# A four-layer decoder on one core: cross-attentions with queries on the partitions, new heads and ends of the expert layers, one context product

## The reference

```python
# l0x and l3x: 16 heads of 8 features, 512 queries against 77 context rows
Q, K, V = split_heads(x @ Wq + bq), split_heads(ctx @ Wk + bk), split_heads(ctx @ Wv + bv)
scores = jnp.einsum('bhqd,bhkd->bhqk', Q, K) / jnp.sqrt(8)     # l0x: mask == 0 -> -1e9 (no biases)
out = merge_heads(jnp.einsum('bhqk,bhkd->bhqd', softmax(scores), V)) @ Wo + bo
# l2x: 8 heads of 64; keys are the 77 context rows (masked) and the 512 tokens
k, v = split(concatenate([ln_x(ctx), ln_l(x)]) @ w_kv); q = ln_l(x) @ w_q * 64 ** -0.5
out = ln_o(merge(softmax(q @ k.T) @ v) @ w_out)
# l1f: top 2 of 8 experts of unlike kinds (width 512), weights by the softmax of nx @ router_w, nx = ln(x)
# l3f: top 2 of 8 experts, weights by the softmax of the two logits, and a shared expert for every token:
shared_out = (silu(x @ sw1) * (x @ sw3)) @ sw2                  # 2 slices of 128
moe_out = sum over the chosen e of cw[e] * ((silu(x @ w1[e]) * (x @ w3[e])) @ w2[e])
```

## Time and profile before

| | us |
|---|---|
| median of 3 runs | 2277.38 (2273.33 to 2279.63) |
| profiled execution | 2252.73 |
| its span, mean granted clock | 2250.9, 0.899 |
| l0x | 158 to 302 |
| l1f | 667 to 1083 |
| l2x | 1155 to 1557 |
| l3x | 1939.9 to 2081.9 |
| l3f | 2082.4 to 2250.9 |
| busy: PE, DVE, ACT, POOL | 1797.8, 1477.1, 1048.0, 393.3 |

### The profile page before, as it was taken

The page is one execution under the profiler, slowest core; times in us unless marked ns, Lnnn a source line. Parts: engine busy times, 40 slices in busy tenths (PEclk is TensorE's granted clock), DMA queues, the critical chain, the costliest instruction groups (busy, mean ns, idle before and its releaser), DMA issues. The chain is left out here.

```text
span 2250.9 us, 34926 instructions
## 1 busy us (share of the span) xinstructions
PE 1797.8 (80%) x12404; PEld 1094.5 (49%) x12521; DVE 1477.1 (66%) x3404; ACT 1048.0 (47%) x2229; POOL 393.3 (17%) x575
## 2 busy tenths in 40 slices
PE   5768967999965999995779999993489889687872
PEld 3445542343334566663556666662245444344661
DVE  4436757888846555555546677686879999566524
ACT  2325534777721333332526555551167777365221
POOL 0110021000023444443110000001200000100374
PEclk8879977999975999998879999996589999799896
DMA  3000000000015588884000000000000000000373
GB/s 86 0 1 1 1 1 0 1 1 1 1 54 212 211 301 300 297 298 146 1 1 1 1 1 1 1 1 17 0 1 2 1 1 2 1 1 1 110 216 115
DMA packets 42797, 134.65 MB, mean 60 GB/s; under 512 B 7117, under 2 KB 22529, under 8 KB 37443
## 3 DMA queue, kind: packets, MB, share of 16 engines
q1 hardware_dynamic: 36587, 121.17, 15.5%
q0 software_dynamic: 4992, 10.23, 1.5%
q10 hardware_dynamic: 1048, 1.01, 0.2%
HBM read 123.29 MB, written 11.45 MB: 60 GB/s over the span
## 5 line engine op out<-in xcount | busy, mean ns | idle before, releaser
L153 POOL TENSOR_SCALAR rstd<-MV 128x2 f32<-128x2 f32 (+1 forms) x100 | 24.4, 244 | 1109.2 <-DVE MV L125 1102.6
L845 DVE TENSOR_REDUCE l1aM<-PS 128x2 f32<-128x1024 f32 x128 | 152.8, 1220 | 22.9 <-PE PS L601 20.8
L763 ACT ACTIVATE l1aE<-PS 128x512 f32<-128x512 f32 x256 | 140.9, 595 | 49.0 <-PE PS L630 45.6
L1575 PE MATMUL PS<-WB,H 128*128 128x512 f32 x312 | 142.6, 600 | 1.2 <-ACT H L1692 1.2
L763 ACT ACTIVATE l3aE<-PS 128x512 f32<-128x512 f32 (+3 forms) x256 | 102.5, 443 | 47.6 <-PE PS L634 44.9
L2463 DVE TENSOR_REDUCE M<-PS 128x1 f32<-128x589 f32 x128 | 92.5, 764 | 36.0 <-PE PS L2274 36.0
L845 DVE TENSOR_REDUCE l3aM<-PS 128x2 f32<-128x256 f32 (+3 forms) x128 | 101.3, 819 | 20.6 <-PE PS L603 19.6
L2372 ACT COPY PT<-PS 128x512 f32<-128x512 f32 x128 | 69.1, 590 | 92.9 <-PE PS L2285 92.6
L2378 ACT ACTIVATE E<-PS,M 128x589 f32<-128x589 f32 x128 | 95.8, 761 | 22.7 <-DVE M L2463 22.6
L1692 ACT ACTIVATE H<-PS,WB 128x128 f32<-128x128 f32 x156 | 44.5, 368 | 121.3 <-PE PS L1566 121.3
L873 DVE SCALAR_TENSOR_TENSOR l3aE<-l3aE,l3aLB 128x2048 f32<-128x2048 f32 (+1 forms) x64 | 94.9, 1483 | 2.7 <-ACT l3aE L763 2.7
(11 more groups left out here) (695 smaller groups left out, 4666.6 us busy)
## 6 DMA issues: line engine op xcount, KB each, us to landing
WB<-in_experts SPq DMA_DIRECT2D x39, 1798.0 KB
TB<-mixed_tails SPq DMA_DIRECT2D x39, 384.0 KB
WB<-in_experts SPq DMA_DIRECT2D x39, 384.0 KB, 4.2
WB<-mixed_out SPq DMA_DIRECT2D x8, 256.0 KB, 4.8
YB<-expert_out SPq DMA_DIRECT2D x8, 256.0 KB, 4.7
WB<-in_fold SPq DMA_DIRECT2D x1, 1676.0 KB, 7.0
cols_l2x_sb<-in_cols_l2x SPq DMA_DIRECT2D x1, 1154.0 KB, 10.2
mixed_tails<-in_tails SPq DMA_DIRECT2D x1, 1152.0 KB, 8.7
```

The costliest lines, as they stand in the source:

```text
L763: nc.scalar.activation(E[0:kn, home(m, kt) + j, q0:S], PS[0:kn, 4 + n % 2, q0:S], ACT.Exp, scale=SCALE).then_inc(exp_done, 1)
L845: v.tensor_reduce(M[:, m % 2, qt, 2 * hp:2 * hp + 2], PS[:, bank:bank + 2, 0:kc], AX, ALU.max, negate=True).then_inc(pair_free, 1)
L1575: mm(o, H1[:, i % 3, c * P:(c + 1) * P], mid_w(i, c), start=(c == 0), stop=False)
```

## The change

**1. l0x and l3x** call a new function, `cross_attention`. Queries are on the partitions. Keys of a batch are spread into `KS`, in which each of eight slots of 77 columns keeps only one head's rows; a score unit S is four float32 matmuls of 64 queries with 308 columns (four heads of 77), one in each quadrant of the array. VectorE takes the maximum and adds it, ScalarE the exponential over 616 columns, X transposes it (8 per unit), O multiplies with V and a column of ones (nine moving columns per head), and VectorE divides. The mask is added on PE by two bf16 matmuls. Nothing is gathered or split.

```diff
+CROSS = (
+    (("X", 1, 0, 0), ("X", 1, 0, 1), ("S", 2, 0), ("O", 0), ("X", 1, 1, 0), ("X", 1, 1, 1), ("S", 2, 1)),
...
+def cross_attention(k, name, w, mask=None):
...
+                        if mask is not None:
+                            mm(PS[:, 2 * (n % 2) + g, 0:CW], k.ident_b, mask[:, qt:qt + 1, :].broadcast_to([P, HG, SC]), start=True, stop=False,
...
+                    for half in range(2):
+                        for g in range(2):
+                            c0, rows = qt * P + 64 * half, slice(64 * g, 64 * g + 64)
+                            ins = mm(PS[64 * half:64 * half + 64, 2 * (n % 2) + g, 0:CW], Q[rows, b % 2, c0:c0 + 64],
+                                     KS[rows, b, HG * p:HG * p + HG, :].rearrange("p j n -> p (j n)"), start=mask is None, stop=True,
...
+                elif kind == "X":
...
+                    for j in range(HG):
+                        ins = nc.tensor.transpose(PS[0:SC, 4 + g, j * P:(j + 1) * P], E[:, n % 2, g, j, :], k.ident)
...
+                    for p in range(2):
+                        for g in range(2):
+                            for j in range(HG):
+                                h = HG * (p + 2 * g) + j
+                                ins = mm(PS[:, 6, h * DA:(h + 1) * DA], ET[:, (2 * i + p) % 4, HG * g + j, :], Va[:, b, h, :], start=True, stop=True)
...
+                    v.tensor_reduce(top[:, s], sc, AX, ALU.max, negate=True).then_inc(maxed, 1)
...
+                    v.tensor_tensor(E[:, s], sc, top[:, s].unsqueeze(3).broadcast_to([P, 2, HG, SC]), ALU.add).then_inc(shifted, 1)
...
-            attention16(k, "l0x", W["l0x"], k.CT, (mask_b[:, :, :], maskT_b[:, :]))
+            cross_attention(k, "l0x", W["l0x"], mask_b[:, :, :])
...
-            attention16(k, "l3x", W["l3x"], k.CT)
+            cross_attention(k, "l3x", W["l3x"])
```

```diff
+            pe.wait_ge(marked, 1)
+            disp.count_tensor(COUNTS, counted)
             pe.wait_ge(centred, 2)
-            pe.wait_ge(scaled, 3)
+            pe.wait_ge(scaled, 2)
...
-            pe.wait_ge(marked, 1)
-            disp.count_tensor(COUNTS, counted)
-            pe.wait_ge(spread, 1)
             pe.wait_ge(lowered, 1)
-            disp.list_tensor(LIST, listed)
+            disp.list_tensor(pe, LIST, spread, listed)
...
+            act.wait_ge(fold_in, 16)
+            for q in range(8):
+                ins = nc.scalar.mul(gd[:, q, :], fold["down"][:, q * P:(q + 1) * P], fold["g1"][:, q:q + 1])
+            ins.then_inc(scaled, 1)
...
+        step(v.tensor_tensor(self.high[:, :, :], self.at_tile[:, :, :],
+                             self.ids_b[:, :].unsqueeze(2).broadcast_to([P, 2 * N, T]), ALU.mult))
+        for c in range(2):
+            own = slice(c * N, (c + 1) * N)
+            v.tensor_tensor(self.at_row[:, own, :], self.iota_b[:, :].unsqueeze(1).broadcast_to([P, N, P]),
+                            self.row_b[:, own].unsqueeze(2).broadcast_to([P, N, P]), ALU.is_equal).then_inc(spread, 1)
```

```diff
+    shared = [u for b in range(BT) for u in (("up", b, 0), ("up", b, 1), ("down", b, 0), ("down", b, 1))]
+    between = {2 * n: u for n, u in enumerate(shared)}
...
+                if i in between and i:
+                    what, b, c = between[i]
+                    (shared_up if what == "up" else shared_down)(b, c)
                 down(i)
```

```diff
-                    for par, c0 in enumerate((0, S - SC)):
-                        o = PS[:, at_ + 1, c0:c0 + SC]
-                        mm(o, Q[:, b % 2, pp, q], Kc[:, b % 2, pp, par, 0:SC], start=True, stop=False)
-                        mm(o, k.ones_b, k.kmask_b[:, b, 0:SC], start=False, stop=True)
+                    mm(context(s), Q[:, b % 2, pp, q], Kc[:, b % 2, pp, :, 0:SC], start=True, stop=False)
+                    mm(context(s), k.ones_b, k.kmask_b[:, b, 0:SC].unsqueeze(1).broadcast_to([P, 2, SC]), start=False, stop=True)
...
+    for n in range(NG // NT):
+        for i, ts in enumerate(((0, 1), (2,), (3,), (4,)) if n < NG // NT - 1 else (range(5),)):
+            values[NT * n + 5 + i] = (n, ts)
```

More of the change, by code:

```diff
@@ L1672, in _ @@
             nc.scalar.activation(pr[:, :, :], pr[:, :, :], ACT.Exp).then_inc(exped, 1)
-            act.wait_ge(scaled, 4)
+            for a, n in enumerate(("s1bb", "b1")):
+                for q in range(8):
+                    ins = nc.scalar.mul(rep[:, a, q, :], k.ones, fold[n][:, q:q + 1])
+            ins.then_inc(scaled, 1)
+            disp.spread_scalar(act, tiled, lowered)
+            act.wait_ge(cleared, 2)
             act.wait_ge(tail_ready, 2)
@@ L1713, in _ @@
                     take(i + 2)
+            act.wait_ge(o_taken, T)
+            for j in range(RING):
+                act.wait_ge(scattered[j], 16 * len(range(j, T, RING)))
+            for b in range(BT):
+                lo = B * S + b * S
+                act.dma_start(yb(1, b), placed[lo:lo + S, :].rearrange("(t p) d -> p t d", p=P)).then_inc(back[b], 16)
             for b in range(BT):
@@ L2205, in ring, with context @@
             return (2 * s + par) % RING
+        def context(s):
+            both = PS[:, slot(s) + 1:slot(s) + 3, :].rearrange("p a n -> p (a n)")
+            return both[:, 0:2 * (S - SC)].rearrange("p (a n) -> p a n", a=2)[:, :, 0:SC]
         @block.tensor
@@ new lines, in shared_down @@
+            def shared_down(b, half):
+                pe.wait_ge(eo_done, 2 * b + 2)
+                if half == 0:
+                    if b:
+                        pe.wait_ge(y_done, b)
+                    else:
+                        pe.wait_ge(known, 1)
+                for t in (2 * half, 2 * half + 1):
+                    for c in range(2):
+                        ins = mm(PS[:, 7, t * P:(t + 1) * P], EO[:, c, t * P:(t + 1) * P], w["w2"][:, c * P:(c + 1) * P],
+                                 start=(c == 0), stop=(c == 1))
+                ins.then_inc(d_ready, 1)
@@ new lines, in turn, with up @@
+            def turn(i):
+                pe.wait_ge(gathered[i % XRING], 16 * (i // XRING + 1))
+                if i:
+                    pe.wait_ge(x_taken, i)
+                nc.tensor.transpose(PS[:, 6, 0:P], XG[:, i % XRING, :], k.ident).then_inc(x_turned, 1)
+            def up(i):
+                pe.wait_ge(loaded[i % RING], 16 * (i // RING + 1))
+                pe.wait_ge(x_taken, i + 1)
+                if i >= 2:
+                    pe.wait_ge(h_done, i - 1)
+                for c in range(4):
+                    ins = mm(PS[:, i % 2, c * P:(c + 1) * P], WB[:, i % RING, c * P:(c + 1) * P], XGT[:, i % 2, :], start=True, stop=True)
+                ins.then_inc(gu_ready, 1)
@@ L2677, in _ @@
                     take(i + 2)
-            act.wait_ge(pair_spread, 1)
-            nc.scalar.activation(pw[:, 1, :], pw[:, 0, :], ACT.Exp).then_inc(exped, 1)
+                if i in between and i and between[i][0] == "up":
+                    shared_gate(*between[i][1:])
+            for j in range(RING):
+                act.wait_ge(scattered[j], 16 * len(range(j, T, RING)))
+            for b in range(BT):
+                lo = B * S + b * S
+                act.dma_start(YB[:, 1, b * NT:(b + 1) * NT, :], placed[lo:lo + S, :].rearrange("(t p) d -> p t d", p=P)).then_inc(back[b], 16)
         @block.vector
@@ L2738, in result, with share @@
                 v.tensor_copy(O[:, i % RING, :], PS[:, 4 + i % 2, 0:P]).then_inc(o_taken, 1)
+            def share(i):
+                what, b, c = between[i]
+                if what == "up":
+                    shared_hidden(b, c)
+                elif c == 1:
+                    shared_out(b)
             for i in range(T):
@@ L2743, in _ @@
                     result(i - 1)
+                    if i in between:
+                        share(i)
             result(T - 1)
@@ L2752, in _ @@
             for b in range(BT):
+                dve.wait_ge(y_done, b + 1)
                 dve.wait_ge(back[b], 32)
```

485 lines of the change are left out of this document (312 added, 173 removed), and 2 rows, old and new, of the table CROSS.

## The result

The changed kernel takes 2308.15 us (median of 4, 2300.84 to 2316.26), the kernel before, on the same chip, 2276.34. The ratio is 1.0140, 95% interval 1.0102 to 1.0179: slower. Forecast were 2305 and slower.

A forecast was written before the change was run, and what follows sets the result against it. PE was taken to bound the cross-attentions and the latent attention. +23 +32 -9.6 -6.5 -11 = +27.9 on the profiled 2252.73 gave 2280.6, plus 24.65 to the runs' median: 2305 us; range 2240 to 2345.

The forecast's parts named there:

- Cross-attentions, the work: Both cross-attentions: 7.56 us of PE work per tile, stages of 137 and 146 us at full clock, -5 and +2.
- Cross-attentions, the clock: Both cross-attentions: narrow output matmuls lower PE's mean clock to 0.81, stages of 165 and 176 us, +23 and +32.
- Rival A: Cross-attentions: the clock holds at 2.4 GHz through the outputs; -30, 2247 us, faster; chance 0.28.
- B: Cross-attentions: the clock never rises, since scores come in pieces of 1.7 us; 2498 us; chance 0.09.
- First expert layer: Its head: fold product on ScalarE, count ahead of fold matmuls, list in halves, return loads on two queues; -9.6 us.
- the return loads: Expert layers: return loads on two queues save 0.5 us in the first, and 0.5 in the last.
- Last layer: Last expert layer: shared work moved from the head to beside POOL, list in halves, earlier count, return loads; -6.5 us.
- the first scatter's 1.66 us: Last expert layer: the first scatter's 1.66 us wait for an output delayed by the shared work goes.
- Latent attention: Latent attention: shorter context scores over 64 steps, less losses at the end and ahead of them; -11 us.
- One matmul of 154 columns and one for the mask cost about 0.44: Latent attention: context scores fall from 0.70 us a step to about 0.44, 16.6 us over 64 steps.
- The values' product streams the same columns, so I count no gain there: Latent attention: the grouped product with the values gains nothing; its last group behind the last scores costs 2.5 us.
- The 24.65 us that the sum adds: Whole kernel: the profiled execution lies 24.65 us under the runs' median of 2277.38, added to 2280.6 to give 2305.

The follow-up runs named there:

- the wide outputs: Changed kernel with each cross-attention output matmul streaming 126 columns instead of 9, results wrong: 2251.47 us, ratio 0.9908 to the kernel before.
- the repeat: The changed kernel run again unaltered for a second trace: 2312.30 us against 2272.44 for the kernel before, ratio 1.0162.
- experiments 9 and 10: Kernel before with only the latent attention's merged context score: 2269.09 us, ratio 0.9984; with the whole latent change and nothing else: 2251.30, ratio 0.9999.
- experiment 5: Changed kernel with a tile's 16 output matmuls in four pieces between transposes and scores: 2256.73 us, ratio 1.0036 to the kernel before.

## Why the prediction was right

**Cross-attentions, the work: right.** All-fast stages of 137 and 146 us were priced; the wide outputs gave 136.7 and 142.2. PE's tile was 7.75 where 7.56 was summed; no wait appeared inside tiles.

**Cross-attentions, the clock: right, and it decides the sign.** Means of 0.81 and 0.77 (0.79 and 0.78 in the repeat), without 10 us at the start and 8 at the end of a stage, against 0.81 taken; +26 and +26 against +32 and +23. That the value came so near is luck: it was read from a stretch of the old stage with other matmuls, in which PE was idle for 2.56 of 20 us, and no row tied it to the new one. That the clock falls with few columns while PE is busy was an inference from two cold stretches; the wider outputs show it. The rule of the Trainium skill ("TensorE: Matmul & The Clock Gate", "HAM oscillation — how this bites in real kernels"), which puts the fall down to idle gaps, does not cover this case: the clock was 0.67 where PE was busy 20.00 of 20 us. Rival A, which followed it, is out; so is B, since the clock came back in every tile or two.

**First expert layer: right.** 400.6 for 410.6, forecast 9.6. In the trace after, the router's end came earlier than priced (712.27, 11.9 us behind the fold's landing, 19.3 before; forecast 4.8 saved, measured 7.4), because most of the eight-column matmuls behind the fold sums found a fast clock. Two errors cancel in the stage: up to the first gather it gained 11.6 us (46.3 from the first matmul before, 34.7 after) where 9.1 were priced; from there to the last scatter it takes 329.7 us for 328.4 (326.5 to 330.7 in the other executions), and the return loads, priced at 0.5, gave nothing (35.9 us from the last scatter to the next stage before, 36.2 after).

**Last layer: the step was right, the size too large on the faster chips.** 4 us there, 7 on the slower one; 6.5 forecast. The head gave 4.1 (31.9 us from the first matmul to the first gather before, 27.8 after), and the shared work is hidden under POOL. What was too large is the rest: of the first scatter's 1.66 us the loop gained 0.2 to 1.2 (98.9 to 99.9 us against 100.1), and the return loads gave nothing (36.4 us from the last scatter to the end, 36.9 after). The first trace alone reads as lost cover, 22 us; the old layer's 124.3 on a slower chip refutes it.

**Latent attention: the failed step.** "One matmul of 154 columns and one for the mask cost about 0.44" measured 0.53, so a step gains 0.17 and not 0.26. "The values' product streams the same columns, so I count no gain there" holds, but it cost: 3.3 us at the end (2.5 priced), in every trace. In the steps the merged score's 8.1 shrank to 6.2 in six of the ten traces and not in the others (experiments 9 and 10), so a loss of 2 there is not shown; of the 16.6 us priced for the steps 6 to 11 came. In the trace of the changed kernel PE's idle time ahead of the context scores grew from 14.2 to 19.4 us:

```profile
L2533 PE MATMUL PS<-K3c,Q 128*128 128x154 f32 x128 | 32.3, 335 | 19.4 <-DVE PT L2739 14.4 <-DVE Va L2692 4.2 <-ACT Va L2622 0.7
```

That is -3 by this trace, as by six of the ten (-7 in three, -9 in one), and nothing beyond 3 us by the runs of it alone, for -11: at the near one of the bounds (-18 and -3) or past it.

The cross stages cost 35 to 50 us by the runs and were priced at 55; the rest saves 13 and was priced at 27. The two errors point opposite ways, so part of the nearness of 2305 is luck. The 24.65 us that the sum adds had no reason beside them. The last layer's 25 us between the chips (193.8 and 168.4 for the old one) are that size; since the result came from a slower chip too, the sum was right to add them.

## What to carry to other kernels

Before an arrangement replaces wide matmuls by many narrow ones, price it at both clocks: here the count of weight loads set its time, and the columns that it streamed the speed of everything around it. Where the loads fill the time anyway, widening the moving side with columns that get overwritten costs next to nothing (0.07 us a tile) and can keep the clock: here it turned +1.4% into -1.0%. And compare a stage across traces only after a second trace has shown how much of it belongs to the chip.

## What the runs showed of the hardware

- At the fast clock a record of the output matmuls (77 x 128 weights, float32) takes 0.112 us with 9 columns, 0.113 with 63 and 0.115 with 126 (medians of the runs of 32 records; the fastest with 9 is 0.109).
- At 9 columns the mean clock of the stages (starts and ends left out) was 0.77 to 0.81, at 63 it was 0.87 to 0.88, at 126 0.99 to 1.00, with PE busy all the time in each.
- Spread narrow work can hold either level for long: 1.00 from 1970 to 1990, 0.59 to 0.63 from 1990 to 2030, with the same kind of tiles (experiment 5).
- Some chips fed the last layer's loop at 153 to 158 GB/s, others at 190 to 193: 121 to 124 us against 99 to 100.
